# Scores of the first query block in one plain 32-bit product of 128 columns instead of three passes over 256

## The chip, the core and the metric

The kernel runs on one core of a Trainium2 chip. The metric is the device time of one execution in microseconds, as the median of several runs. Lower is better.

## What is computed

One transformer layer in 32-bit floats for 2 batches of 512 tokens of width 512. After a layer norm (`xn`) three things are added up: the input, the output of an attention, and the output of a mixture of experts with a shared expert. The attention has 32 query heads in 8 groups; each group of 4 shares one key and value head of size 128:

```python
q = q * cos + rotate_half(q) * sin          # the same for k
scores = einsum('bkgtd,bksd->bkgts', qg, k) / sqrt(128)
scores = where(causal, scores, -inf)
attn = softmax(scores, axis=-1)
out = einsum('bkgts,bksd->bkgtd', attn, v)  # then the product with Wo
```

The mask is causal, so queries 0 to 127 of a batch see keys 0 to 127 only. Each token also goes through 2 of 16 experts (512 to 128 and back), chosen by a router.

## The kernel before

The five engines run one instruction stream each and meet at semaphores; the order of each stream is written out by hand in its own function `key_head(g)`, which stands once for g = 0, as the body of a loop for g = 1 to 6, and once for g = 7. One key head means: 4 query heads of both batches (b = 0 and 1), the projections that the next steps need, and 4 or 5 tiles of 128 expert rows.

**Split products.** Most products are made from split operands. ScalarE (or GpSimd) writes the value rounded to the type fp32r (`_hi`), VectorE writes the rest (`_lo`), and TensorE adds three passes, lo x hi, hi x lo and hi x hi (`product`, line 1241). The experts' products (lines 1460 and 1477) are plain 32-bit ones: one call of matmul, which the trace shows as two records. The transpositions (lines 1369, 1395, 1450, 1469) are one record per call.

**Queries.** For one batch and head, TensorE projects q transposed (`project_q`, line 1323: 128 dimensions x 512 tokens) into the bank PROJ_BANK. VectorE multiplies it by the cosine and sine tables (`turn_q1`, `turn_q2`, lines 919 and 931; semaphore q_turned). GpSimd adds the two halves in place (`add_q`, line 429; q_summed). ScalarE writes q_hi (`hi_q`, line 579; q_hi_ok), VectorE q_lo (`lo_q`, line 939; q_split). The next `turn_q1` waits for q_summed and q_split, because the tile `rot` is used again. For the first batch of key head 0 the sum is made by VectorE (line 1024). The bank PROJ_BANK also takes the next key and value projection (`project_kv`, line 1345), which waits for q_turned of the head before.

**Keys.** `project_kv` gives keys and values, VectorE turns the keys (`turn_k`), GpSimd sums them (`add_k`), TensorE transposes them back into PROJ_BANK (`transpose_k`, line 1362), ScalarE writes kT_hi (`hi_kT`, line 594) and VectorE kT_lo (`lo_kT`, line 968; kT_split). Two places on TensorE wait for kT_split: the first scores of a batch, and the third query projection (h = 2, line 1335), which needs the bank back. In the order of TensorE that projection is line 1542 for b = 1 and line 1625 for b = 0 of the next head.

**Scores.** `scores(g, b, i, m)` (line 1372) makes the scores of query block i (128 queries) against the keys 0 to 128 (i + 1) - 1. Two heads share a bank for i = 0 and 1, one head has it for i = 2 and 3; each such share is a use, and the uses take turns between two banks. For i = 0 the kernel computes 256 columns of which 128 are read afterwards. Then VectorE adds the mask and takes the maximum (`maxima`, line 975), ScalarE makes the exponentials (`exps`, line 600), VectorE the inverse sums (line 985), GpSimd normalises (`normalise`, line 463), TensorE transposes the probabilities (`transpose_p`, line 1387; prob_ok), they are split (lines 624 and 1008), multiplied with the values (`values`, line 1399) and projected (`project_out`, line 1412).

The four uses of the first query block in a key head stand at lines 1486 and 1496 (b = 0) and 1559 and 1576 (b = 1) of TensorE's order. Around the first and third of them that order reads:

```python
project_q(g + 1, 0, 3, 3)      # 1642, the end of the loop body
values(g, 1, 2, 1)
values(g, 1, 2, 2)
scores(g, 0, 0, 0)             # 1486, the start of the next one
project_kv(g, 1, 0, 0)         # 1487
...
scores(g, 1, 0, 0)             # 1559
project_out(g, 0, 1, 0)
values(g, 0, 2, 2)
transpose_p(g, 0, 3, 0)        # 1562
```

Of the kernel before, what the change touches and what calls it, by code (L numbers as in the profile page):

```python
# [7 lines left out]
F32 = mybir.dt.float32  # L8
F32R = mybir.dt.float32r
BF16 = mybir.dt.bfloat16  # L10
I32 = mybir.dt.int32
ALU = mybir.AluOpType
ACT = mybir.ActivationFunctionType
AX_X = mybir.AxisListType.X

P = 128
B, T, D = 2, 512, 512
# [4 lines left out]
G = HEADS // KV  # L22
# [13 lines left out]
S_BANKS, MOE_BANK, PROJ_BANK, OUT_BANK, PT_BANKS, OT_BANK = (0, 1), 2, 3, 4, (5, 6), 7  # L36
# [5 lines left out]
SHARE = [((0, 1), (2, 3)), ((0, 1), (2, 3)), ((0,), (1,), (2,), (3,)), ((0,), (1,), (2,), (3,))]  # L42
USES = 12
USE0 = [0, 2, 4, 8]
# [10 lines left out]
def wait_count(eng, sem, value):  # L55

    if not isinstance(value, int) or value > 0:
        eng.wait_ge(sem, value)


def count(per_step, g, b, k):

    return (2 * per_step) * g + (per_step * b + k)
# [7 lines left out]
def no_head(g):  # L71

    return isinstance(g, int) and not 0 <= g < KV
# [7 lines left out]
def build(nc, x, wq, wkv, wo, shared, sb3, w12, w3, b12, b3, router_w, router_b, router_bias,  # L81
# [8 lines left out]
    with ExitStack() as ctx:  # L90
        def sb(name, shape, dt=F32, stack=ctx):
            return stack.enter_context(nc.sbuf_tensor(name, shape, dt))

        def sem(name):
            return ctx.enter_context(nc.semaphore(name))
# [13 lines left out]
        bank = [ctx.enter_context(nc.psum_tensor(f"bank{i}", [P, 512], F32)) for i in range(8)]  # L109
# [65 lines left out]
            wo_raw = sb("wo_raw", [P, G, D], stack=raws)  # L175
        wo_lo = sb("wo_lo", [P, G, D], F32R)
        wo_hi = sb("wo_hi", [P, G, D], F32R)
        q_hi = sb("q_hi", [P, B, G, T], F32R)
        q_lo = sb("q_lo", [P, B, G, T], F32R)
        kT_hi = sb("kT_hi", [P, B, T], F32R)  # L180
        kT_lo = sb("kT_lo", [P, B, T], F32R)
        v_hi = sb("v_hi", [P, B, TB, P], F32R)
        v_lo = sb("v_lo", [P, B, TB, P], F32R)
        rot = sb("rot", [P, 2, T])
# [35 lines left out]
        q_psum, q_turned, q_summed, q_hi_ok, q_split = (sem(n) for n in ("q_psum", "q_turned", "q_summed", "q_hi_ok", "q_split"))  # L220
# [169 lines left out]
        def _(pool):  # L390
# [38 lines left out]
            def add_q(g, b, h):  # L429

                if no_head(g):
                    return
                pool.wait_ge(q_turned, count(4, g, b, h + 1))
                wait_count(pool, q_split, count(4, g, b, h))
                nc.gpsimd.tensor_tensor(rot[:, 0, :], rot[:, 0, :], rot[:, 1, :], ALU.add).then_inc(q_summed, 1)  # L435

            def add_k(g, b, i):

# [112 lines left out]
        def _(act):  # L551
# [3 lines left out]
            for n in range(B * HC):  # L555
                c, b = n % HC, n // HC
# [4 lines left out]
            for j in range(B):  # L561
                last = nc.scalar.activation(lT[:, j * T:(j + 1) * T], bank[LT_BANKS[j]][0:E, :], ACT.Copy)
# [6 lines left out]
            for t in range(4):  # L569
                s, b = t % 2, t // 2  # L570
# [8 lines left out]
            def hi_q(g, b, h, turned=rot):  # L579
                if no_head(g):  # L580
                    return
                act.wait_ge(q_summed, count(4, g, b, h + 1))
                nc.scalar.activation(q_hi[:, b, h, :], turned[:, 0, :], ACT.Copy).then_inc(q_hi_ok, 1)

            def hi_v(g, b, i, at=PROJ_BANK):
                if no_head(g):
# [7 lines left out]
            def hi_kT(g, b, at=PROJ_BANK):  # L594
                if no_head(g):
                    return
                act.wait_ge(kT_psum, count(1, g, b, 1))
                nc.scalar.activation(kT_hi[:, b, :], bank[at][:, :], ACT.Copy).then_inc(kT_hi_ok, 1)

            def exps(g, b, i, m):  # L600
# [164 lines left out]
        def _(dve):  # L765
# [9 lines left out]
            for n in range(NB):  # L775
                dve.wait_ge(x_in[n], 16)
                last = nc.vector.bn_stats(stats[:, n, :], y[:, n, :])
            link(last)
            for n in range(NB):
                last = nc.vector.bn_aggr(mv[:, n, :], stats[:, n, :])  # L780
# [17 lines left out]
            for n in range(B * HC):  # L798
                c, b = n % HC, n // HC
# [131 lines left out]
            def turn_q2(g, b, h, at=PROJ_BANK, turned=rot):  # L931
                if no_head(g):
                    return

                q = bank[at]
                nc.vector.tensor_tensor(turned[0:64, 1, :], q[64:128, :], qs[64:128, :], ALU.mult)
                nc.vector.tensor_tensor(turned[64:128, 1, :], q[0:64, :], qs[0:64, :], ALU.mult).then_inc(q_turned, 1)  # L937

            def lo_q(g, b, h, turned=rot):
                if no_head(g):  # L940
                    return
                dve.wait_ge(q_hi_ok, count(4, g, b, h + 1))
                nc.vector.tensor_tensor(q_lo[:, b, h, :], turned[:, 0, :], q_hi[:, b, h, :].bitcast(F32), ALU.subtract)\
                    .then_inc(q_split, 1)

            def turn_k(g, b, i, at=PROJ_BANK):
# [68 lines left out]
            for h in range(G):  # L1015
                turned = first_rot[h % 2]
                turn_q1(0, 0, h, FIRST_Q_BANKS[h], turned)
                turn_q2(0, 0, h, FIRST_Q_BANKS[h], turned)
                if h > 0:
                    lo_q(0, 0, h - 1, first_rot[(h - 1) % 2])  # L1020
                if h == 2:
                    lo_kT(0, 0, FIRST_KT_BANK)
                dve.wait_ge(q_turned, h + 1)
                nc.vector.tensor_tensor(turned[:, 0, :], turned[:, 0, :], turned[:, 1, :], ALU.add).then_inc(q_summed, 1)
            lo_q(0, 0, TB - 1, first_rot[1])

            def last_lo_q(g, b):
# [212 lines left out]
        def _(pe):  # L1240
            def product(dst, terms, stop=True):

                for k, (a_hi, a_lo, c_hi, c_lo) in enumerate(terms):
                    nc.tensor.matmul(dst, a_lo, c_hi, start=k == 0, stop=False)  # L1244
                    nc.tensor.matmul(dst, a_hi, c_lo, start=False, stop=False)  # L1245
                    last = nc.tensor.matmul(dst, a_hi, c_hi, start=False, stop=stop and k == len(terms) - 1)  # L1246
                return last
# [3 lines left out]
            for n in range(B * HC):  # L1251
                c, b = n % HC, n // HC
                pe.wait_ge(xn_ready, TB * (b + 1))
                wait_count(pe, xT_ok, n - 3)
                for k in range(TB):
                    last = nc.tensor.transpose(bank[TR_BANKS[n % 4]][:, k * P:(k + 1) * P],
                                               xn[:, TB * b + k, c * P:(c + 1) * P], ident[:, :])
# [3 lines left out]
            for b in range(B):  # L1261
                span = slice(b * T, (b + 1) * T)
                last = product(bank[LT_BANKS[b]][0:E, :],
                               [(rw_hi[:, c, :], rw_lo[:, c, :], xT_hi[:, c, span], xT_lo[:, c, span])
                                for c in range(HC)])
# [105 lines left out]

            def scores(g, b, i, m):

                use, width = USE0[i] + m, max(256, P * (i + 1))
                if i == 0 and m == 0:
                    pe.wait_ge(kT_split, count(1, g, b, 1))
                if i == 0:
                    pe.wait_ge(q_split, count(4, g, b, SHARE[i][m][-1] + 1))
                wait_count(pe, exps_ok, count(USES, g, b, use - 1))
                cols = slice(i * P, (i + 1) * P)  # L1380
                for k, h in enumerate(SHARE[i][m]):
                    s = bank[S_BANKS[use % 2]]
                    last = product(s[:, 256 * k:256 * k + width],
                                   [(q_hi[:, b, h, cols], q_lo[:, b, h, cols], kT_hi[:, b, 0:width], kT_lo[:, b, 0:width])])
                last.then_inc(s_psum, 1)

            def transpose_p(g, b, i, j):
# [262 lines left out]
            last = (KV - 1, 1, TB - 1)  # L1650
# [85 lines left out]
```

## Time and profile before

| | us |
|---|---|
| median of 3 runs | 976.89 (973.25 to 977.38) |
| the profiled execution | 974.4 |
| span of its instructions | 972.6 |
| PE busy | 922.1 (95%) |
| PE weight loads busy | 772.5 (79%) |
| DVE busy | 678.7 (70%) |
| POOL busy | 391.5 (40%) |
| ACT busy | 377.3 (39%) |

PE is TensorE's matmuls and PEld its weight loads, which overlap them; DVE is VectorE, ACT ScalarE, POOL GpSimd, SP the queue that issues most DMAs. Matmuls are pipelined and their ends are modelled, so the duration of a record holds a latency that overlaps the next one. For how long a matmul keeps the engine, the distance between two starts is the figure to read. Register, branch and semaphore instructions are not counted as busy.

### The profile page before, as it was taken

The page shows a single profiled execution, that of the slowest core. Times are in us where ns is not written, and L with a number is a line of the kernel's source. Part 1 is how long each engine was busy: PE and PEld are TensorE (multiplying, and loading weights), DVE is VectorE, ACT ScalarE, POOL GpSimd, SP SyncE. Part 2 cuts the span into 40 slices and gives each one's busy share as a digit, 9 for nine tenths or more (in the row PEclk, how much of TensorE's full clock was granted, in tenths as well). Part 3 has the DMA queues.
Part 4 walks back from the last instruction along what each step waited for, and adds up shares of the span by engine and source line. Part 5 has one row for each costly group of instructions (what it writes and reads, how often), then busy time and mean ns, then how long its engine had stood idle before and what let it go on. Part 6 is the DMA issues. An engine that isn't in the chain of part 4 may idle for free.

```text
span 972.6 us, 16710 instructions
## 1 busy us (share of the span) xinstructions
PE 922.1 (95%) x4945; PEld 772.5 (79%) x4945; DVE 678.7 (70%) x1543; ACT 377.3 (39%) x997; POOL 391.5 (40%) x510
## 2 busy tenths in 40 slices
PE   2799799999999999999999999999999999999986
PEld 2477678887888888888888888888888988888864
DVE  7486785758665775768666585757767586657884
ACT  2111343435333443435434443335433453334532
POOL 5900277624352353324362253425343243423571
PEclk9989899999999999999999999999999999999999
DMA  9700221224233243215323142414423242321160
GB/s 323 279 0 1 77 76 65 101 73 149 82 96 89 81 145 110 84 42 166 105 87 96 54 151 91 125 38 145 127 84 92 64 144 77 114 70 55 43 186 32
DMA packets 51727, 97.70 MB, mean 100 GB/s; under 512 B 5872, under 2 KB 17776, under 8 KB 51696
## 3 DMA queue, kind: packets, MB, share of 16 engines
q1 hardware_dynamic: 49136, 88.94, 28.8%
q0 software_dynamic: 2560, 8.39, 2.7%
q8 instruction: 15, 0.25, 0.1%
q14 instruction: 16, 0.13, 0.0%
HBM read 74.76 MB, written 22.54 MB: 100 GB/s over the span
## 4 chain that ended last, share of the span: by engine, by line
PE 83%; DVE 11%; issue 2%; DMA 1%; POOL 1%; ACT 1%; SPq 0%; DVEq 0%; ACTq 0%; POOLq 0%
PE bank L1244 7%; PE bank L1246 7%; PE bank L1245 7%; PE bank L1395 6%; PE bank L1339 6%; PE bank L1423 6%; PE bank L1341 6%; PE bank L1340 6%; PE bank L1460 6%; PE bank L1425 6%; PE bank L1424 6%; PE bank L1408 3%; PE bank L1410 3%; PE bank L1409 3%; PE bank L1477 3%
## 5 line engine op out<-in xcount | busy, mean ns | idle before, releaser
L469 POOL TENSOR_SCALAR prob<-prob,rsum 128x128 f32<-128x128 f32 (+3 forms) x256 | 138.7, 560 | 307.7 <-DVE rsum L987 307.6
L624 ACT ACTIVATE pT_hi<-bank 128x512 fp32r<-128x512 f32 x160 | 94.7, 599 | 185.1 <-PE bank L1395 118.1
L605 ACT ACTIVATE prob<-bank,nmax 128x128 f32<-128x128 f32 (+3 forms) x256 | 133.0, 525 | 52.2 <-DVE nmax L981 52.2
L435 POOL TENSOR_TENSOR rot<-rot 128x512 f32<-128x512 f32 x60 | 77.2, 1287 | 171.3 <-DVE rot L937 171.3
L981 DVE CUSTOM_DVE_ANT_0 bank<-bank,causal 128x128 f32<-128x128 f32 (+3 forms) x256 | 122.0, 503 | 32.3 <-PE bank L1246 31.9
L1008 DVE TENSOR_TENSOR pT_lo<-bank,pT_hi 128x512 fp32r<-128x512 f32 x160 | 107.7, 683 | 45.8 <-ACT pT_hi L624 45.5
L1339 PE MATMUL bank<-xT_hi,wq_lo 128*128 128x512 f32 x256 | 109.9, 429 | 6.1 <-DVE v_lo L965 6.1
L1423 PE MATMUL bank<-wo_hi,oT_lo 128*128 128x512 f32 x256 | 109.2, 427 | 3.4 <-DVE oT_lo L993 2.8
L1341 PE MATMUL bank<-xT_hi,wq_hi 128*128 128x512 f32 x256 | 101.4, 396 | 0.0
L1340 PE MATMUL bank<-xT_lo,wq_hi 128*128 128x512 f32 x256 | 101.3, 396 | 0.0
L1425 PE MATMUL bank<-wo_hi,oT_hi 128*128 128x512 f32 x256 | 101.0, 395 | 0.0
L1424 PE MATMUL bank<-wo_lo,oT_hi 128*128 128x512 f32 x256 | 100.8, 394 | 0.0
L1244 PE MATMUL bank<-kT_hi,q_lo 128*128 128x256 f32 (+2 forms) x256 | 89.4, 349 | 3.1 <-ACT prob L605 2.1
L1395 PE MATMUL bank<-ident,prob 128*128 128x128 f32 x640 | 87.1, 274 | 3.9 <-POOL prob L469 3.7
L1395 PEld LDWEIGHTS bank<-ident,prob 128*128 128x128 f32 x640 | 73.9, 141 | 13.8 <-POOL prob L469 7.2
L1245 PE MATMUL bank<-kT_lo,q_hi 128*128 128x256 f32 (+2 forms) x256 | 82.9, 324 | 0.0
L1246 PE MATMUL bank<-kT_hi,q_hi 128*128 128x256 f32 (+2 forms) x256 | 82.9, 324 | 0.0
L1244 PE MATMUL bank<-wkv_hi,xT_lo 128*128 128x256 f32 x256 | 75.9, 297 | 2.2 <-DVE prob L937 1.6
L1245 PE MATMUL bank<-wkv_lo,xT_hi 128*128 128x256 f32 x256 | 72.3, 282 | 0.0
L1246 PE MATMUL bank<-wkv_hi,xT_hi 128*128 128x256 f32 x256 | 72.1, 282 | 0.0
L1408 PE MATMUL bank<-pT_hi,v_lo 128*128 128x512 f32 x160 | 66.8, 418 | 1.5 <-DVE pT_lo L1008 1.5
L615 ACT ACTIVATE oT_hi<-bank 128x512 fp32r<-128x512 f32 x64 | 38.3, 599 | 76.6 <-PE bank L1410 76.6
(183 smaller groups left out, 2025.6 us busy)
## 6 DMA issues: line engine op xcount, KB each, us to landing
w_raw<-w SPq DMA_DIRECT2D x31, 512.0 KB, 3.8
wq_raw<-wq SPq DMA_DIRECT2D x32, 256.0 KB, 3.3
wo_raw<-wo SPq DMA_DIRECT2D x32, 256.0 KB, 3.2
xg<-x_slots SPq DMA_DIRECT2D x31, 256.0 KB, 2.6
eb<-b SPq DMA_DIRECT2D x31, 256.0 KB, 4.3
w_raw<-w SPq DMA_DIRECT2D x31, 256.0 KB, 4.1
y_slots<-moe_y SPq DMA_DIRECT2D x31, 256.0 KB, 3.1
x_slots<-pairs SPq DMA_DIRECT2D x3, 2048.0 KB, 16.2
```

The costliest lines, as they stand in the source:

```text
L469: last = nc.gpsimd.tensor_scalar(row, row, rsum[:, G * i + h:G * i + h + 1], 1.0, ALU.mult, ALU.mult)
L605: last = nc.scalar.activation(prob[i % 2][:, h, 0:P * (i + 1)], bank[S_BANKS[use % 2]][:, 256 * k:256 * k + P * (i + 1)], ACT.Exp, bias=nm ...
L1244: nc.tensor.matmul(dst, a_lo, c_hi, start=k == 0, stop=False)
L1245: nc.tensor.matmul(dst, a_hi, c_lo, start=False, stop=False)
L1246: last = nc.tensor.matmul(dst, a_hi, c_hi, start=False, stop=stop and k == len(terms) - 1)
L1339: nc.tensor.matmul(q, wq_lo[:, h, col], xT_hi[:, c, span], start=c == 0, stop=False)
L1340: nc.tensor.matmul(q, wq_hi[:, h, col], xT_lo[:, c, span], start=False, stop=False)
L1341: last = nc.tensor.matmul(q, wq_hi[:, h, col], xT_hi[:, c, span], start=False, stop=c == HC - 1)
L1395: last = nc.tensor.transpose(bank[PT_BANKS[n % 2]][:, h * P:(h + 1) * P], prob[i % 2][:, h, j * P:(j + 1) * P], ident[:, :])
L1423: nc.tensor.matmul(dst, oT_lo[:, k, h], wo_hi[:, h, :], start=h == 0, stop=False)
L1424: nc.tensor.matmul(dst, oT_hi[:, k, h], wo_lo[:, h, :], start=False, stop=False)
L1425: last = nc.tensor.matmul(dst, oT_hi[:, k, h], wo_hi[:, h, :], start=False, stop=h == G - 1)
```

## The change

It gives the first query block its own operands, `q_first` and `k_first`, in plain 32-bit floats and 128 columns wide, and makes its scores in one matmul call per head of 128 x 128 x 128 instead of three passes over 256 columns. The sum of the turned query becomes two operations (the first 128 tokens into `q_first`, the other 384 in place), q_hi and q_lo shrink to 384 tokens, ScalarE makes one more copy per batch and key head, ahead of kT_hi, and the waits move: block 0 waits for q_summed, block 1 takes the wait for q_split.

```diff
--- before.py
+++ after.py
@@ -175,8 +175,10 @@
             wo_raw = sb("wo_raw", [P, G, D], stack=raws)
         wo_lo = sb("wo_lo", [P, G, D], F32R)
         wo_hi = sb("wo_hi", [P, G, D], F32R)
-        q_hi = sb("q_hi", [P, B, G, T], F32R)
-        q_lo = sb("q_lo", [P, B, G, T], F32R)
+        q_first = sb("q_first", [P, B, G, P])
+        k_first = sb("k_first", [P, B, P])
+        q_hi = sb("q_hi", [P, B, G, T - P], F32R)
+        q_lo = sb("q_lo", [P, B, G, T - P], F32R)
         kT_hi = sb("kT_hi", [P, B, T], F32R)
         kT_lo = sb("kT_lo", [P, B, T], F32R)
         v_hi = sb("v_hi", [P, B, TB, P], F32R)
@@ -432,7 +434,8 @@
                     return
                 pool.wait_ge(q_turned, count(4, g, b, h + 1))
                 wait_count(pool, q_split, count(4, g, b, h))
-                nc.gpsimd.tensor_tensor(rot[:, 0, :], rot[:, 0, :], rot[:, 1, :], ALU.add).then_inc(q_summed, 1)
+                nc.gpsimd.tensor_tensor(q_first[:, b, h, :], rot[:, 0, 0:P], rot[:, 1, 0:P], ALU.add)
+                nc.gpsimd.tensor_tensor(rot[:, 0, P:T], rot[:, 0, P:T], rot[:, 1, P:T], ALU.add).then_inc(q_summed, 1)
 
             def add_k(g, b, i):
 
@@ -580,7 +583,7 @@
                 if no_head(g):
                     return
                 act.wait_ge(q_summed, count(4, g, b, h + 1))
-                nc.scalar.activation(q_hi[:, b, h, :], turned[:, 0, :], ACT.Copy).then_inc(q_hi_ok, 1)
+                nc.scalar.activation(q_hi[:, b, h, :], turned[:, 0, P:T], ACT.Copy).then_inc(q_hi_ok, 1)
 
             def hi_v(g, b, i, at=PROJ_BANK):
                 if no_head(g):
@@ -595,6 +598,7 @@
                 if no_head(g):
                     return
                 act.wait_ge(kT_psum, count(1, g, b, 1))
+                nc.scalar.activation(k_first[:, b, :], bank[at][:, 0:P], ACT.Copy)
                 nc.scalar.activation(kT_hi[:, b, :], bank[at][:, :], ACT.Copy).then_inc(kT_hi_ok, 1)
 
             def exps(g, b, i, m):
@@ -940,7 +944,7 @@
                 if no_head(g):
                     return
                 dve.wait_ge(q_hi_ok, count(4, g, b, h + 1))
-                nc.vector.tensor_tensor(q_lo[:, b, h, :], turned[:, 0, :], q_hi[:, b, h, :].bitcast(F32), ALU.subtract)\
+                nc.vector.tensor_tensor(q_lo[:, b, h, :], turned[:, 0, P:T], q_hi[:, b, h, :].bitcast(F32), ALU.subtract)\
                     .then_inc(q_split, 1)
 
             def turn_k(g, b, i, at=PROJ_BANK):
@@ -1021,7 +1025,9 @@
                 if h == 2:
                     lo_kT(0, 0, FIRST_KT_BANK)
                 dve.wait_ge(q_turned, h + 1)
-                nc.vector.tensor_tensor(turned[:, 0, :], turned[:, 0, :], turned[:, 1, :], ALU.add).then_inc(q_summed, 1)
+                nc.vector.tensor_tensor(q_first[:, 0, h, :], turned[:, 0, 0:P], turned[:, 1, 0:P], ALU.add)
+                nc.vector.tensor_tensor(turned[:, 0, P:T], turned[:, 0, P:T], turned[:, 1, P:T], ALU.add)\
+                    .then_inc(q_summed, 1)
             lo_q(0, 0, TB - 1, first_rot[1])
 
             def last_lo_q(g, b):
@@ -1371,17 +1377,22 @@
 
             def scores(g, b, i, m):
 
-                use, width = USE0[i] + m, max(256, P * (i + 1))
+                use, width = USE0[i] + m, P * (i + 1)
                 if i == 0 and m == 0:
                     pe.wait_ge(kT_split, count(1, g, b, 1))
                 if i == 0:
+                    pe.wait_ge(q_summed, count(4, g, b, SHARE[i][m][-1] + 1))
+                if i == 1:
                     pe.wait_ge(q_split, count(4, g, b, SHARE[i][m][-1] + 1))
                 wait_count(pe, exps_ok, count(USES, g, b, use - 1))
-                cols = slice(i * P, (i + 1) * P)
+                cols = slice((i - 1) * P, i * P)
                 for k, h in enumerate(SHARE[i][m]):
-                    s = bank[S_BANKS[use % 2]]
-                    last = product(s[:, 256 * k:256 * k + width],
-                                   [(q_hi[:, b, h, cols], q_lo[:, b, h, cols], kT_hi[:, b, 0:width], kT_lo[:, b, 0:width])])
+                    s = bank[S_BANKS[use % 2]][:, 256 * k:256 * k + width]
+                    if i == 0:
+                        last = nc.tensor.matmul(s, q_first[:, b, h, :], k_first[:, b, :], start=True, stop=True)
+                    else:
+                        last = product(s, [(q_hi[:, b, h, cols], q_lo[:, b, h, cols],
+                                            kT_hi[:, b, 0:width], kT_lo[:, b, 0:width])])
                 last.then_inc(s_psum, 1)
 
             def transpose_p(g, b, i, j):
```

## Rows read from the trace of the kernel before

**Rows 1.** The page: busy time, share of the span, instructions; the chain that ended last.

```profile
PE 922.1 (95%) x4945; PEld 772.5 (79%) x4945; DVE 678.7 (70%) x1543; ACT 377.3 (39%) x997; POOL 391.5 (40%) x510
...
PE 83%; DVE 11%; issue 2%; DMA 1%; POOL 1%; ACT 1%; SPq 0%; DVEq 0%; ACTq 0%; POOLq 0%
```

**Rows 2.** Busy time by stretches of the span (window, its length, engines, clock, DMA).

```profile
420.00:530.00 110.00, 109.92 (x600) 93.14 (x599) 75.86 (x179) 46.00 (x125) 41.29 (x56) 1.00 0.31 98
```

**Rows 3.** Timeline at line 1486, key head 3: start, us, engine, operation [idle before <-releaser].

```profile
416.32 0.69 DVE L929 TENSOR_TENSOR rot<-bank,qc 128x512 f32<-128x512 f32 x1 [1.02 <-PE bank L1341]
...
417.51 0.28 PE L1244 MATMUL bank<-kT_hi,q_lo 128*128 128x256 f32 x1
417.51 0.19 PEld L1245 LDWEIGHTS bank<-kT_lo,q_hi 128*128 128x128 f32 x1
...
417.63 0.19 PEld L1246 LDWEIGHTS bank<-kT_hi,q_hi 128*128 128x128 f32 x1
417.73 0.68 DVE L937 TENSOR_TENSOR rot<-bank,qs 64x512 f32<-64x512 f32 x1
...
418.11 0.28 PE L1246 MATMUL bank<-kT_hi,q_hi 128*128 128x256 f32 x1
...
418.46 0.19 PEld L1244 LDWEIGHTS bank<-wkv_hi,xT_lo 128*128 128x128 f32 x1 [0.28 <-DVE rot L937]
418.46 0.39 PE L1244 MATMUL bank<-wkv_hi,xT_lo 128*128 128x256 f32 x1
...
418.69 0.29 PE L1245 MATMUL bank<-wkv_lo,xT_hi 128*128 128x256 f32 x1
```

**Rows 4.** TensorE's instructions grouped by line and form: count | busy us, mean ns | idle.

```profile
L1395 PE MATMUL bank<-ident,prob 128*128 128x128 f32 x640 | 87.1, 274 | 3.9 <-POOL prob L469 3.7
...
L1460 PE MATMUL bank<-w_raw,xgT 128*128 128x256 f32 x248 | 59.7, 383 | 0.0
...
L1460 PEld LDWEIGHTS bank<-w_raw,xgT 128*128 128x128 f32 x248 | 45.5, 189 | 8.2 <-ACT xgT L650 2.1
```

**Rows 5.** Timeline: the experts' up projection, eight records in one.

```profile
422.66 1.89 PE L1460 MATMUL bank<-w_raw,xgT 128*128 128x256 f32 x8
```

**Rows 6.** Timeline around the keys of the second batch, key head 3 (lines 1536 to 1542).

```profile
452.56 1.28 POOL L435 TENSOR_TENSOR rot<-rot 128x512 f32<-128x512 f32 x1 [1.15 <-DVE rot L937]
...
453.65 1.04 PE L1395 MATMUL bank<-ident,prob 128*128 128x128 f32 x8
453.85 0.60 ACT L650 ACTIVATE xgT<-bank 128x512 f32<-128x512 f32 x1 [5.46 <-PE bank L1450]
...
454.34 0.59 ACT L598 ACTIVATE kT_hi<-bank 128x512 fp32r<-128x512 f32 x1
...
454.82 0.63 ACT L583 ACTIVATE q_hi<-rot 128x512 fp32r<-128x512 f32 x1
...
454.97 0.69 DVE L972 TENSOR_TENSOR kT_lo<-bank,kT_hi 128x512 fp32r<-128x512 f32 x1 [0.58 <-ACT kT_hi L598]
...
455.71 0.19 PEld L1339 LDWEIGHTS bank<-xT_hi,wq_lo 128*128 128x128 f32 x1
```

**Rows 7.** The other engines' instructions grouped by line and form.

```profile
L435 POOL TENSOR_TENSOR rot<-rot 128x512 f32<-128x512 f32 x60 | 77.2, 1287 | 171.3 <-DVE rot L937 171.3
...
L943 DVE TENSOR_TENSOR q_lo<-rot,q_hi 128x512 fp32r<-128x512 f32 x62 | 52.0, 838 | 13.8 <-ACT q_hi L583 13.7
...
L442 POOL TENSOR_TENSOR ksum<-krot 128x256 f32<-128x256 f32 x32 | 23.8, 742 | 36.1 <-DVE krot L957 36.1
...
L667 ACT ACTIVATE hT<-bank 128x128 f32<-128x128 f32 x31 | 8.5, 275 | 0.0
```

**Rows 8.** Timeline at line 1562, key head 3.

```profile
466.63 3.13 POOL L469 TENSOR_SCALAR prob<-prob,rsum 128x512 f32<-128x512 f32 x4 [1.24 <-DVE rsum L987]
...
469.97 0.37 PEld L1395 LDWEIGHTS bank<-ident,prob 128*128 128x128 f32 x2
```

**Rows 9.** Who waited for whom: total us, times, longest us.

```profile
ACT q_hi L583 <- POOL rot L435: 5.6, 8, 0.8
```

## What the change does to the time: the prediction

> **What bounds the kernel now.** I read the page first. TensorE is busy 95% of the span and the chain that ended last lies on it for 83% [rows 1]. That busy share overstates the load, since ends are modelled, so I took the table by stretches next: in the steady key heads PE is busy 109.92 of 110.00 us, the weight loads 93.14, and VectorE (75.86), ScalarE (46.00) and GpSimd (41.29) have room; the granted clock there is 1.00, which is the 2.4 GHz level [rows 2]. The reader is to see a kernel bound by the order of work on TensorE, with the other engines idle a third of the time or more. The last view is the timeline of one steady key head (the one that runs from about 418 to 529 us), read for the places where TensorE's next instruction waits for another engine. There are few: the largest is 0.28 us [rows 3]. So TensorE work removed should come off the end, except inside a stretch that a fixed path through another engine covers. The question is how much TensorE time goes, and how many of the places lie in such a stretch.
>
> **TensorE: what goes and what comes.** The scores of the first query block are 64 head products (2 batches, 32 heads), issued two by two in 32 uses of a bank, four per key head (lines 1486, 1496, 1559, 1576). Today each head is three instructions of 256 columns. A record shows 0.28 to 0.30 us but they overlap; what counts is the distance of starts: from 417.51 to 418.11 us are five distances, 0.12 each [rows 3]. A use of six records occupies 0.72 us.
>
> A plain 32-bit product appears in the trace as two records per call: the experts' up projection has 248 for its 31 x 4 calls, 383 ns mean [rows 4]. A group of 8 takes 1.89 us [rows 5]; less one record of 0.383 that leaves 1.51 for 7 distances, 0.215 each. Half the columns give 0.108. Eight 128-column transposes, also from 32-bit data, take 1.04 us, and less one record's 0.274 that is 0.109 per record [rows 4, 6]. So the new head is 2 x 0.109 = 0.22 us, and a use 0.44 instead of 0.72: 0.28 us saved. Weight loads could spoil this: a plain load's record is 189 ns long [rows 4]. But loads of 0.19 us start every 0.12 us under the present passes [rows 3], so 0.12 per record is the near bound: a use of 0.48, saving 0.24. The far bound is in the rivals. I take 0.28, since nothing shows a load limit at 0.12 rather than the streaming. All 32 uses: 9.0 us, or 7.7 at the near bound.
>
> **The use at line 1486 gives nothing.** The following key and value projection (line 1487) writes the projection bank and waits until VectorE has turned the last query head. VectorE starts at 416.32, having waited for TensorE's projection, needs three operations of 0.69 and ends at 418.41; the load for line 1487 starts at 418.46 after 0.28 idle [rows 3]. That path starts ahead of the score product and does not contain it, so a shorter product is only a longer wait. Eight uses, 8 x 0.28 = 2.2 us, are lost. The others leave 24 x 0.28 = 6.7 us.
>
> **The new copy of the keys.** ScalarE writes k_first ahead of kT_hi, 16 times. A 128-column copy out of PSUM takes 275 ns; successive ScalarE records overlap by 0.10 (an operation of 0.60 at 453.85, the next at 454.34), so kT_hi comes 0.17 later [rows 6, 7]. For the second batch that chain is tight: kT_hi at 454.34, kT_lo on VectorE from 454.97 to 455.66, and the load of the third query projection (line 1542) at 455.71, 0.05 after its release [rows 6]. It has perhaps 0.07 of play, as a load runs ahead of its matmul. A wait also costs more than itself: after the one at 418.46 the next record starts 0.23 later where 0.12 is usual [rows 3]. So 0.10 + 0.10 = 0.20 us per key head, 1.6 in all; bounds 0 (the shorter q_lo, queued ahead, gives it back) and 0.3 x 8 = 2.4. Behind kT_lo on VectorE queue q_lo and the maxima of the last query block, which have more room. For the first batch line 1625 comes later in the order and I cost the copy at nothing.
>
> **The next wait uncovered.** After the use at line 1559 comes the transposition of the last block's probabilities (line 1562). GpSimd ends normalising them at 466.63 + 3.13 = 469.76, the load starts at 469.97 [rows 8]. TensorE 0.28 earlier would be there 0.07 before the release, plus 0.05 for the signal: some 0.1 us, 0.8 in all (bounds 0 and 0.25 x 8 = 2.0). The uses at lines 1496 and 1576 have no releaser that close behind, other than ones whose own source lies after the use and moves with it.
>
> **The small edits.** GpSimd's sum of the turned query becomes two operations. From 256 columns at 742 ns and 512 at 1287, an operation has 197 fixed, so the split costs 0.20 us, 60 times [rows 7]. I cost it at nothing: the sum that ends at 452.56 + 1.28 = 453.84 is read by ScalarE at 454.82, nearly 1 us later [rows 6], and ScalarE waited for that sum 8 times, 5.6 us in all [rows 9]. Going the other way, q_hi and q_lo lose 128 of 512 columns, about 0.1 of 0.63 and 0.2 of 0.84 us [rows 6, 7], mostly off the path. The same split on VectorE in the prologue (4 times, under 0.1 each) is paid by the shorter q_lo. The first block's scores wait for the sum instead of the split, which comes earlier; the second block takes over the wait for the split and is behind it already. Nothing is moved on SP and no DMA changes.
>
> **Sum.** 6.7 - 1.6 - 0.8 = 4.3, less 0.3 for the first and last key heads, where TensorE waits for others more: 4.0 us. The profiled execution took 974.4 (span 972.6): 970.4. The median of three runs is 976.89, 2.5 above it, which would give 972.9. Between the two I say 971.5. That is 0.4%, just under the 0.5% that can be told from no change here (about 4.9 us).
>
> **The rivals.** (1) All three open uses reach the end, because the shorter q_lo and q_hi repay the copy and line 1562: -6.7, 967.7 to 970.2 by the two baselines. For: GpSimd, ScalarE and VectorE have room [rows 2]. Against: the 0.05 at line 1542 [rows 6]. Chance 0.22.
>
> (2) The gain melts: every kept use runs into some wait on VectorE within the key head, as at line 1487. Then only the copy is felt, -1 to +1.6, some 976. For: VectorE's waits stand close behind TensorE's in the order. Against: only 0.08 us of 110 is idle [rows 2]. Chance 0.13.
>
> (3) Slower through the sum on GpSimd: if each of the 60 sums passed its 0.20 to q_split and so to VectorE's next turn, 12 us stand against 6.7, +5.3, 979.7 to 982. It decides once ScalarE reaches q_hi less than 0.2 us after the sum; the trace shows 1 us [rows 6]. Chance 0.05.
>
> (4) Slower through weight loads: if a plain 128-column record had to pay its load openly, it costs 0.189 + 0.109 = 0.30, a head 0.60 instead of 0.36, and 64 heads +15 us, about 991. It decides at 0.18 per record. The experts' records hide such loads under 0.215, and the present passes under 0.12 [rows 3, 5]. Chance 0.05. The Trainium skill (TensorE: Matmul & The Clock Gate, Part 3, The mechanism) says that a load overlaps running matmuls only where the row group differs; with 107 ns per load of 128 columns (its section LDWEIGHTS, an estimate from its P / 1.2) a head would be 4 x 107 = 0.43 and the change a loss of some 4.5 us. By that rule the present passes of full height could not be 0.12 apart with a load each, so the trace contradicts it.
>
> **How the numbers follow.** The forecast case, -1.5 to -6.5 us, has 0.55; about 0.18 of it lies beyond -4.9. With rival 1 that makes faster 0.40. Same: 0.37 + 0.13 = 0.50. Slower: 0.10. The range runs from rival 1 on the lower baseline, 967.7, less 1.2 for the spread of the runs (the lowest, 973.25, against 974.4), so 966, to rival 2 with the full price of the copy on the upper baseline, 976.89 + 1.6, so 979. Rivals 3 and 4 lie outside it, with the far tails of the others.
>
> **What would show it.** Right: the first block's records as 128 matmuls of 128 columns, about 0.11 apart and 0.44 per use; the wait at line 1487's load grown from 0.28 to about 0.55; a wait of 0.1 to 0.2 on kT_lo at the third query projection; a period of key heads shorter by about 0.5 us (0.84 - 0.20 - 0.10). Wrong: records 0.2 or more apart; a period unchanged or shorter by 0.8; ScalarE's q_hi waiting for GpSimd far more than 8 times.

## The result and the profile after

The changed kernel takes 970.89 us (median of 20 runs, 968.62 to 974.52) against 974.85 for the kernel before (20 runs beside them, 970.96 to 977.38). The ratio is 0.9962, 95% interval 0.9951 to 0.9973: about 3.7 us faster. The profiled execution took 969.35, its span is 967.6. Of all executions below one, of pool_twice, fell into a slower state (1036.41 us at a granted clock of 0.845, where the others have 0.98 to 1.00) and is left out of its ratio.

The page of the changed kernel, busy times and the chain (before: [rows 1]):

```profile
PE 913.9 (94%) x4881; PEld 762.9 (79%) x4881; DVE 672.7 (70%) x1547; ACT 373.2 (39%) x1013; POOL 395.9 (41%) x570
...
PE 80%; DVE 13%; issue 3%; ACT 2%; DMA 1%; POOL 1%; SPq 0%; DVEq 0%; ACTq 0%; another core or an unknown queue 0%; POOLq 0%
```

TensorE has 64 records fewer (192 passes gone, 128 come), and the chain has moved a little from TensorE to VectorE and ScalarE. The groups by line and form of the changed kernel show the new instructions (before: [rows 4, 7]):

```profile
L1392 PE MATMUL bank<-k_first,q_first 128*128 128x128 f32 x128 | 19.5, 274 | 0.7 <-DVE kT_lo L976 0.7
L1392 PEld LDWEIGHTS bank<-k_first,q_first 128*128 128x128 f32 x128 | 19.0, 190 | 3.6 <-DVE kT_lo L976 1.1
...
L437 POOL TENSOR_TENSOR q_first<-rot 128x128 f32<-128x128 f32 x60 | 27.8, 464 | 174.4 <-DVE rot L941 174.4
...
L438 POOL TENSOR_TENSOR rot<-rot 128x384 f32<-128x384 f32 x60 | 60.6, 1010 | 0.0
...
L947 DVE TENSOR_TENSOR q_lo<-rot,q_hi 128x384 fp32r<-128x384 f32 x62 | 46.5, 750 | 12.1 <-ACT q_hi L586 11.9
...
L601 ACT ACTIVATE k_first<-bank 128x128 f32<-128x128 f32 x16 | 4.4, 274 | 38.9 <-PE bank L1375 38.9
```

The timeline of the changed kernel at the start of key head 3 (before: [rows 3]):

```profile
416.56 0.69 DVE L933 TENSOR_TENSOR rot<-bank,qc 128x512 f32<-128x512 f32 x1 [1.26 <-PE bank L1347]
...
417.75 0.61 PE L1392 MATMUL bank<-k_first,q_first 128*128 128x128 f32 x4
417.97 0.68 DVE L941 TENSOR_TENSOR rot<-bank,qs 64x512 f32<-64x512 f32 x1
...
418.71 0.19 PEld L1250 LDWEIGHTS bank<-wkv_hi,xT_lo 128*128 128x128 f32 x1 [0.54 <-DVE rot L941]
...
418.93 0.29 PE L1251 MATMUL bank<-wkv_lo,xT_hi 128*128 128x256 f32 x1
```

Four records take 0.61 us; less one record of 0.274, three distances are 0.112 each. The wait of the key and value projection has grown from 0.28 to 0.54 us: what the shorter product gave is in it.

At the three other uses the gain stays. I compared, position by position in TensorE's order, the starts in both traces from the second to the last key head: at the instruction behind each of these uses the changed kernel moves ahead by 0.28 (line 1496), 0.26 to 0.27 (line 1559) and 0.27 us (line 1576), in every head. The distance between key heads shows it too. These are the loads with which key head 1 and key head 7 begin, first in the kernel before, then in the changed one:

```profile
193.86 0.19 PEld L1244 LDWEIGHTS bank<-kT_hi,q_lo 128*128 128x128 f32 x1
...
862.97 0.19 PEld L1244 LDWEIGHTS bank<-kT_hi,q_lo 128*128 128x128 f32 x1
```

```profile
195.65 0.19 PEld L1392 LDWEIGHTS bank<-k_first,q_first 128*128 128x128 f32 x1
...
859.68 0.19 PEld L1392 LDWEIGHTS bank<-k_first,q_first 128*128 128x128 f32 x1
```

A sixth of the difference is the period of a key head: 111.52 us before, 110.67 after, 0.85 less. I use this period below, as it leaves out the first and the last head, where single profiles scatter: in the kernels of this study that share the old product (before, fill_before, width128) the first head alone took 98.4 to 100.7 us.

### The profile page after: what moved, and what is told of

It is laid out like the page before. It is cut to its first block, busy times and chain, and to the rows that moved or that the text cites. A ratio compares the mean times of both kernels' runs of the same rounds, so it can differ in the third digit from the quotient of the medians.

```text
span 967.6 us, 16670 instructions
## 1 busy us (share of the span) xinstructions
PE 913.9 (94%) x4881; PEld 762.9 (79%) x4881; DVE 672.7 (70%) x1547; ACT 373.2 (39%) x1013; POOL 395.9 (41%) x570
## 4 chain that ended last, share of the span: by engine, by line
PE 80%; DVE 13%; issue 3%; ACT 2%; DMA 1%; POOL 1%; SPq 0%; DVEq 0%; ACTq 0%; another core or an unknown queue 0%; POOLq 0%
PE bank L1250 7%; PE bank L1252 7%; PE bank L1251 6%; PE bank L1406 6%; PE bank L1471 6%; PE bank L1434 6%; PE bank L1436 5%; PE bank L1435 5%; PE bank L1345 5%; PE bank L1347 5%; PE bank L1346 5%; PE bank L1419 3%; PE bank L1421 3%; PE bank L1420 3%; PE bank L1488 3%
## 5 line engine op out<-in xcount | busy, mean ns | idle before, releaser
L472 POOL TENSOR_SCALAR prob<-prob,rsum 128x128 f32<-128x128 f32 (+3 forms) x256 | 136.7, 554 | 296.7 <-DVE rsum L991 296.6
L437 POOL TENSOR_TENSOR q_first<-rot 128x128 f32<-128x128 f32 x60 | 27.8, 464 | 174.4 <-DVE rot L941 174.4
L1250 PE MATMUL bank<-kT_hi,q_lo 128*128 128x256 f32 (+2 forms) x192 | 71.9, 374 | 3.7 <-issue 2.0
L1345 PEld LDWEIGHTS bank<-xT_hi,wq_lo 128*128 128x128 f32 x256 | 48.6, 190 | 20.9 <-DVE v_lo L969 8.2
L1252 PE MATMUL bank<-kT_hi,q_hi 128*128 128x256 f32 (+2 forms) x192 | 64.8, 337 | 0.0
```

The source lines that it names most:

```text
L472: last = nc.gpsimd.tensor_scalar(row, row, rsum[:, G * i + h:G * i + h + 1], 1.0, ALU.mult, ALU.mult)
L1345: nc.tensor.matmul(q, wq_lo[:, h, col], xT_hi[:, c, span], start=c == 0, stop=False)
```

## The experiments

Each ran in five rounds (width128 in three) against the kernel before. "Ratio" is to that kernel, "period" the mean of six key heads of one profiled execution, from the same two loads as above. The kernels ran in three groups, in which the kernel before had medians of 974.29 (after_again, both twice kernels, fill_after), 974.76 (copy_twice, no_copy, pool_twice, long_split) and 974.08 us (the others); across groups the ratio is the figure to compare.

| kernel | median us | ratio (95% interval) | period us |
|---|---|---|---|
| before | 974.85 | | 111.52 |
| changed | 970.89 | 0.9962 (0.9951 to 0.9973) | 110.67 |
| after_again | 969.36 | 0.9949 (0.9929 to 0.9969) | 110.63 |
| twice_at_wait | 967.55 | 0.9929 (0.9907 to 0.9951) | 110.93 |
| twice_at_open | 971.13 | 0.9967 (0.9951 to 0.9982) | 111.12 |
| fill_after | 965.23 | 0.9902 (0.9880 to 0.9923) | 110.10 |
| copy_twice | 969.58 | 0.9953 (0.9935 to 0.9971) | 110.94 |
| no_copy | 969.47 | 0.9947 (0.9930 to 0.9963) | 110.60 |
| pool_twice | 972.93 | 0.9975 (0.9962 to 0.9988) | 111.01 |
| long_split | 974.71 | 0.9999 (0.9985 to 1.0012) | 111.18 |
| long_swap | 973.40 | 0.9996 (0.9981 to 1.0011) | 110.96 |
| fill_swap | 966.99 | 0.9934 (0.9915 to 0.9952) | 110.18 |
| fill_before | 971.33 | 0.9975 (0.9961 to 0.9989) | 111.25 |
| width128 | 974.00 | 0.9992 (0.9977 to 1.0006) | 111.44 |

**The control, after_again.**

> The changed kernel itself, as the control for the three that run with it. My theory: three of the four first-block uses per key head shorten the time, the one ahead of the key and value projection only lengthens a wait, so 3.5 to 4.5 us under the kernel before.

969.36 us; ratio 0.9949, so 5.0 us under the kernel before, the period 110.63. Changed kernel and control together stand for 3.7 to 5.0.

**Does the use at the start of the head count?**

```diff
+                        for _ in range(2 if (b, m) == (0, 0) else 1):
                             last = nc.tensor.matmul(s, q_first[:, b, h, :], k_first[:, b, :], start=True, stop=True)
```

> Each product of the use at the start of the key head (b = 0, heads 0 and 1) is issued twice, 0.44 us more of TensorE work in each of 8 key heads, the result unchanged. My theory: the wait for VectorE that follows has grown to 0.54 us and takes it up, so the time stays within 0.8 us of the changed kernel and the wait in the profile falls to 0.1. The rival, that TensorE's work is what counts everywhere: 8 x 0.44 = 3.5 us slower than the changed kernel.

967.55 us, not slower than the control: 3.5 us of added TensorE work cost nothing in the time. Its timeline at the same place:

```profile
416.02 1.05 PE L1393 MATMUL bank<-k_first,q_first 128*128 128x128 f32 x8
...
416.98 0.19 PEld L1250 LDWEIGHTS bank<-wkv_hi,xT_lo 128*128 128x128 f32 x1
```

Eight records now, and the load behind them carries no wait mark (a row has one above 0.15 us). The rival (3.5 us slower than the control) is outside the interval. The period is 0.3 above the control's, though, 1.8 us in six key heads. Most of it is the wait for late weights told of at the end; TensorE's waits of 200 to 860 us, the control first:

```profile
PEld bank L1250 <- ACT prob L609: 0.7, 1, 0.7
```

```profile
PEld bank L1250 <- ACT prob L609: 2.2, 3, 1.6
```

**The same work at an open use.**

```diff
+                        for _ in range(2 if (b, m) == (1, 0) else 1):
                             last = nc.tensor.matmul(s, q_first[:, b, h, :], k_first[:, b, :], start=True, stop=True)
```

> The same doubling at the first use of the second batch (heads 0 and 1), where my theory sees no wait behind it: 3.5 us slower than the changed kernel, 3.0 to 3.8 with the small play at the transposition behind it. A rival by which gains and losses there melt into later waits on VectorE: under 1.5 us.

971.13 us, 1.8 over the control, period + 0.49 for 0.44 of work. Position by position all of the 0.45 appears right behind the doubled product. The time, half of the 3.5 expected with an interval of about 2.4 either way, doesn't tell the theories apart alone; the trace speaks for the open use. Against twice_at_wait it is 3.6 us.

**Is the wait real idle time?** The transpositions of the last block's probabilities are ready 2 us before, so they can stand in it.

```diff
                 scores(g, 0, 0, 0)
-                project_kv(g, 1, 0, 0)
                 transpose_p(g - 1, 1, 3, 0)
                 transpose_p(g - 1, 1, 3, 1)
+                project_kv(g, 1, 0, 0)
```

> The changed kernel with the eight transpositions of the last block's probabilities (0.87 us, released 2 us before) issued ahead of the key and value projection instead of behind it, so that TensorE works while VectorE turns the last query. My theory: the 0.54 us wait and the 0.1 that follows a wait go, 8 x 0.55 to 0.65 = 4.4 to 5.2 us faster than the changed kernel. The rival: the key and value projection or its readers are on a path of their own (VectorE's queue), and the wait shows up at the values or the first query projection: under 1.5 us.

965.23 us, 4.1 under the control, a little less than the 4.4 to 5.2 expected and far from the rival; period - 0.53. The timeline:

```profile
416.34 0.61 PE L1392 MATMUL bank<-k_first,q_first 128*128 128x128 f32 x4
...
416.78 1.04 PE L1406 MATMUL bank<-ident,prob 128*128 128x128 f32 x8
...
417.55 0.19 PEld L1250 LDWEIGHTS bank<-wkv_hi,xT_lo 128*128 128x128 f32 x1
```

TensorE does not wait between the three. This is the fastest kernel of the study: ratio 0.9902. The same edit on the kernel before:

> The kernel before with only the transpositions ahead of the key and value projection. Its wait there is 0.28 us and the 0.1 behind it: 8 x 0.37 = 3.0 us faster than before, 971 to 972. If my theory of the wait is wrong, under 1 us.

971.33 us, 2.7 under its runs beside it, ratio 0.9975, so 2.4 by the ratio against 3.0 expected. The smaller wait gives the smaller gain, in line with the theory.

**The copy of the keys, made twice** (the first time into a spare tile) **and left out.**

```diff
+                nc.scalar.activation(k_spare[:, b, :], bank[at][:, 0:P], ACT.Copy)
                 nc.scalar.activation(k_first[:, b, :], bank[at][:, 0:P], ACT.Copy)
```

> The changed kernel with the 128-column copy of the keys made a second time into a spare tile, ahead of the first: kT_hi and kT_lo 0.17 us later, 16 times, the result unchanged. The step of my prediction (0.2 us per key head once the play is used up) gives 1.4 to 2 us slower than the changed kernel. The theory after reading its trace, that the projection waiting for kT_lo is reached 0.13 us or more after it: 0.3 to 1 us.

969.58 us, ratio 0.9953: within the intervals that is the changed kernel. Its trace is not. The period is 0.3 longer than the changed kernel's and its control's (110.94 against 110.67 and 110.63), and a wait has grown; TensorE's waits of 200 to 860 us, the changed kernel first, then copy_twice:

```profile
PEld bank L1345 <- DVE v_lo L969: 1.2, 6, 0.2
```

```profile
PEld bank L1347 <- DVE v_lo L971: 2.7, 12, 0.4
```

So a second copy does reach TensorE, in the one profiled execution (974.79 us, the slowest of the seven). Whether it costs time in the median is not shown.

```diff
-                nc.scalar.activation(k_first[:, b, :], bank[at][:, 0:P], ACT.Copy)
...
-                        last = nc.tensor.matmul(s, q_first[:, b, h, :], k_first[:, b, :], start=True, stop=True)
+                        last = nc.tensor.matmul(s, q_first[:, b, h, :], kT_hi[:, b, 0:P].bitcast(F32), start=True, stop=True)
```

> The changed kernel without the copy of the keys: the product reads the rounded kT_hi as plain 32-bit floats, so the first block's scores lose the low part of the keys. If the copy costs what I predicted, 1.6 us faster than the changed kernel; by the trace, where nothing waits for kT_lo, 0 to 0.5.

969.47 us, ratio 0.9947, period 110.60 against 110.63 to 110.67. The interval of the time alone would still allow the 1.6 us; the period, 0.03 to 0.07 shorter, does not. The first copy costs next to nothing. The timeline of the changed kernel at that place (before: [rows 6]) tells why:

```profile
453.33 1.41 DVE L1041 TENSOR_TENSOR wo_lo<-wo_raw,wo_hi 128x512 fp32r<-128x512 f32 x1
...
454.45 0.27 ACT L601 ACTIVATE k_first<-bank 128x128 f32<-128x128 f32 x1
454.61 0.60 ACT L602 ACTIVATE kT_hi<-bank 128x512 fp32r<-128x512 f32 x1
...
454.79 0.19 PEld L1434 LDWEIGHTS bank<-wo_hi,oT_lo 128*128 128x128 f32 x1 [0.24 <-DVE wo_lo L1041]
...
455.24 0.69 DVE L976 TENSOR_TENSOR kT_lo<-bank,kT_hi 128x512 fp32r<-128x512 f32 x1 [0.50 <-ACT kT_hi L602]
...
456.06 0.19 PEld L1345 LDWEIGHTS bank<-xT_hi,wq_lo 128*128 128x128 f32 x1
```

kT_hi starts 0.16 after the copy, as reckoned. But in this head TensorE is held just before, 0.24 us, by the split of an output weight, and then reaches the projection (456.06) 0.13 after kT_lo is done (455.93). Two waits that stand one behind the other are paid once. In the kernel before, key head 3, which I had read, has no such hold and only 0.05 between kT_lo and the load [rows 6]; key heads 2, 4, 5 and 6 are not like it. Key head 2 of the kernel before:

```profile
343.48 0.69 DVE L972 TENSOR_TENSOR kT_lo<-bank,kT_hi 128x512 fp32r<-128x512 f32 x1 [0.41 <-ACT kT_hi L598]
...
344.42 0.19 PEld L1339 LDWEIGHTS bank<-xT_hi,wq_lo 128*128 128x128 f32 x1
```

The load comes 0.25 after kT_lo is done, and 0.20 to 0.23 after it in key heads 4, 5 and 6: room for the 0.17 of the copy. In the changed kernel that room is used up: in key heads 2, 5 and 6 the load comes 0.05 to 0.06 after kT_lo, but the matmul behind it starts, counted from the first load of the key head, at most 0.03 later than in no_copy.

**GpSimd's sum, made longer.**

```diff
+                nc.gpsimd.tensor_tensor(q_spare[:, h, :], rot[:, 0, 0:P], rot[:, 1, 0:P], ALU.add)
                 nc.gpsimd.tensor_tensor(q_first[:, b, h, :], rot[:, 0, 0:P], rot[:, 1, 0:P], ALU.add)
```

> The changed kernel with GpSimd's first 128-column sum made twice (0.46 us more, 60 times, into a spare tile, result unchanged). My theory: ScalarE comes to the sum 0.9 us after it, so under 1 us slower than the changed kernel, all of it through VectorE being slowed while GpSimd works. The rival of the prediction, that the sums reach VectorE's turns: 5 us and more of 28.

972.93 us, ratio 0.9975: some 2.5 over the changed kernel by the ratios of it and its control, the period 0.34 to 0.38 longer. More than my "under 1", less than the rival's 5. The waits of ScalarE and TensorE show where; first the changed kernel, then pool_twice:

```profile
ACT q_hi L586 <- POOL rot L438: 7.7, 8, 1.0
...
PEld bank L1471 <- ACT xgT L654: 2.9, 11, 0.3
```

```profile
PEld bank L1473 <- ACT xgT L656: 5.4, 12, 0.6
...
ACT q_hi L588 <- POOL rot L440: 12.0, 10, 1.5
...
PEld bank L1347 <- DVE kT_lo L978: 1.5, 6, 0.2
```

ScalarE has to wait for the sum of the fourth query of the second batch, and behind that rounding in its queue stands the copy of the expert's rows, for which TensorE's up projection waits. Against the control that projection comes 0.4 us later in each of key heads 1 to 6, all of the longer period. The waits for kT_lo are new too, but cost nothing: where they stand, the wait for wo_lo just ahead of them is gone.

**The shorter split undone in time.**

```diff
+                nc.scalar.activation(q_pad[:, b, 0, :], turned[:, 0, 0:P], ACT.Copy)
                 nc.scalar.activation(q_hi[:, b, h, :], turned[:, 0, P:T], ACT.Copy).then_inc(q_hi_ok, 1)
...
+                nc.vector.tensor_tensor(q_pad[:, b, 1, :], turned[:, 0, 0:P], turned[:, 0, 0:P], ALU.subtract)
                 nc.vector.tensor_tensor(q_lo[:, b, h, :], turned[:, 0, P:T], q_hi[:, b, h, :].bitcast(F32), ALU.subtract)
```

> The changed kernel with the shortening of the query split undone in time: ScalarE and VectorE each make one more 128-column operation per head into a spare tile (0.17 and 0.2 us, 64 times; result unchanged). If the shorter split is what paid for the copy of the keys, 1 to 2 us slower than the changed kernel, with a wait on kT_lo or on the turned query in the profile. If VectorE has room there, under 0.7 us.

974.71 us, ratio 0.9999: all of the gain is gone, 4 to 5 us, more than either theory allowed. The waits I had named are not there. What grew most is that chain through ScalarE again; the timeline of long_split at the up projection of the third tile:

```profile
473.94 0.31 ACT L587 ACTIVATE q_pad<-rot 128x128 f32<-128x128 f32 x1 [1.23 <-POOL rot L439]
...
474.15 0.51 ACT L588 ACTIVATE q_hi<-rot 128x384 fp32r<-128x384 f32 x1
...
474.57 0.58 ACT L656 ACTIVATE xgT<-bank 128x512 f32<-128x512 f32 x1
...
475.20 1.59 PEld L1474 LDWEIGHTS bank<-w_raw,xgT 128*128 128x128 f32 x8 [0.55 <-ACT xgT L656]
```

GpSimd's sum, ScalarE's pad and rounding, the copy, and TensorE idle for 0.55 us. The pad is an operation of its own and so costs more than the columns the change took off; the run overstates what the shorter split saved, but shows that it was no free term.

**That chain cut.** The next kernel tests it, on the same lengthened split:

```diff
-                last_hi_q(g, 1)
                 copy_xg(tile_of(g, 2))
+                last_hi_q(g, 1)
```

> The kernel with the lengthened query split (long_split), and on ScalarE the copy of the expert's rows (third tile) ahead of the rounding of the fourth query head, not behind it. The trace of long_split shows 0.42 us of its loss per key head at the experts' up projection of that tile, which waits for this copy, which stands behind a rounding that waits for GpSimd's sum. If that chain is the price, 3 to 3.5 us come back: 971 to 972, the key heads 110.7 to 110.8 us apart instead of 111.2. If VectorE's longer split is the price, the wait reappears at the next product and the time stays above 973.5.

973.40 us, ratio 0.9996, a miss. The named wait went back to its old size, and the period fell by 0.22, half of the 0.42:

```profile
PEld bank L1474 <- ACT xgT L656: 2.1, 6, 0.3
```

Totals of this wait are 5.4 us in long_split and 2.1 here. By the ratios the time came down by 0.3 us, which the intervals can't tell from nothing. So this chain is one part of the price of the longer split. Position by position against the control, long_split loses 0.4 us at this up projection in each of key heads 2 to 6 and 0.10 to 0.14 some 88 us into it, where the first load of an output projection waits for oT_lo, which VectorE writes; together that is nearly all of its 0.55 us of longer period. In long_split, key head 3:

```profile
506.23 0.19 PEld L1437 LDWEIGHTS bank<-wo_hi,oT_lo 128*128 128x128 f32 x1 [0.16 <-DVE oT_lo L1000]
```

This second place stays in long_swap in most key heads, so VectorE's part of the longer split has a price as well. Waits of 0.1 to 0.2 on the probabilities and on the output weight's split are longer or more frequent in both traces too. Why the median of long_swap shows none of the 0.22 per key head that its period gives back is open.

> Both orders at once on the changed kernel: the transpositions ahead of the key and value projection (fill_after), and ScalarE's copy of the expert's rows ahead of the fourth query head's rounding. In the changed kernel that second chain costs about 0.1 us per key head, so 0.5 to 1.5 us under fill_after, some 964; the rival, that the next wait takes it, gives the same as fill_after.

966.99 us, ratio 0.9934 against 0.9902, period 110.18 against 110.10: nothing gained over fill_after. In the changed kernel the chain was not worth cutting. By the two ratios this kernel is even 3 us slower, at the edge of what the intervals allow while the periods are nearly equal; so the gain of fill_after may be nearer 3 us than 4.

**Fewer columns alone.**

```diff
-                use, width = USE0[i] + m, max(256, P * (i + 1))
+                use, width = USE0[i] + m, P * (i + 1)
```

> The kernel before with three passes over 128 columns for the first block instead of 256, the result unchanged. No row shows such a pass. If it streams at the rate of the longer ones, 0.06 us per record or 0.11 if the weight load bounds it: 0.18 to 0.33 us per head instead of 0.36, 1 to 8 us faster. If so short a pass runs at the rate of the plain product or slower (0.22 and more per record), 0.66 per head and 64 x 0.3 = 19 us slower, less the 2.4 that the first wait hides.

974.00 us, ratio 0.9992 (0.9977 to 1.0006): 0.8 us faster, not to be told from nothing, and far from the 19 slower. The timeline of this kernel at one use:

```profile
420.00 0.27 PE L1245 MATMUL bank<-kT_lo,q_hi 128*128 128x128 f32 x1
420.11 0.28 PE L1246 MATMUL bank<-kT_hi,q_hi 128*128 128x128 f32 x1
420.22 0.27 PE L1244 MATMUL bank<-kT_hi,q_lo 128*128 128x128 f32 x1
420.33 0.28 PE L1245 MATMUL bank<-kT_lo,q_hi 128*128 128x128 f32 x1
420.44 0.28 PE L1246 MATMUL bank<-kT_hi,q_hi 128*128 128x128 f32 x1
```

The records are 0.11 us apart, where those of 256 columns were 0.12 [rows 3]. That is the upper price of my first case, for which I had said 1 us faster. Halving the columns of a rounded pass gives back next to nothing; the change saves because it has two records per head instead of three.

## Why the prediction was right, and which of its terms were not

I forecast -4.0 us and 971.5; measured are -3.7 by the ratio (-5.0 in the control) and 970.89.

- **The price of the new product** held: 0.112 per record against 0.109, no load limit, so rival 4 is out. A use takes 0.44 to 0.45 us, and 0.26 to 0.28 came off where 0.28 was said.
- **The use at line 1486** gives nothing, as said: the wait grew by 0.26 us, doubling the product was free, and work moved into the wait came off the time. This is the best supported step.
- **The other three uses** reach the end. 3 x 0.27 = 0.81 against a period shorter by 0.85; I had forecast 0.5 for the period after the two costs below, and had named "a period unchanged or shorter by 0.8" as a sign of being wrong. By that sign the sum for the middle heads was wrong, though the total was right.
- **The copy of the keys** was mis-sized: 1.6 us forecast, nothing found in no_copy's period and trace. The delay of 0.17 was right; that it would reach TensorE was not. I had taken the play from key head 3, where it is 0.05; in four other key heads it is 0.20 to 0.25, in three of them because TensorE is held by wo_lo just before. The expected wait of 0.1 to 0.2 on kT_lo does not show. By the trace of copy_twice a second copy would not have been free.
- **Line 1562** I put at 0.8 us. The load there is released just in time now (in key head 3 GpSimd is done at 470.01, the load starts at 470.06), but no loss of 0.1 shows in the period. Together with the copy, 2.4 us of cost were forecast that did not come.
- **GpSimd's longer sum**, costed at nothing because ScalarE came 1 us later in the head I read, does lie on a path at one place, the fourth query of the second batch. Its wait total went from 5.6 [rows 9] to 7.7 us. In the changed kernel ScalarE's shorter rounding (526 ns, before 0.63 us [rows 6]) covers about half of the 0.2. I had looked at one place in the key head and spoken for all eight.
- **The shorter split**, which I called mostly off the path, was worth more than I said: lengthened again, the gain was gone. How much it is worth by itself is not shown, since that run makes the split longer than it was.
- **First and last key head** I put at -0.3. By the period, 8 x 0.85 = 6.8 us should have come, and 3.7 to 5.0 did, so some 2 to 3 us are missing outside the six middle heads. The profiles say the same: outside them passed 303.5, 304.5 and 304.0 us in the three with the old product (before, fill_before, width128) and 303.6, 304.9 and 304.3 in the changed kernel, its control and no_copy. One part of the loss is shown. In the first key head TensorE stands 6 us for VectorE's v_lo. The first load of the head and the load behind that wait, in the kernel before and then in the changed one:

```profile
95.47 0.19 PEld L1244 LDWEIGHTS bank<-kT_hi,q_lo 128*128 128x128 f32 x1 [1.34 <-DVE kT_lo L972]
...
122.23 0.29 PEld L1339 LDWEIGHTS bank<-xT_hi,wq_lo 128*128 128x128 f32 x1 [6.02 <-DVE v_lo L965]
```

```profile
96.26 0.52 PEld L1392 LDWEIGHTS bank<-k_first,q_first 128*128 128x128 f32 x4 [1.13 <-DVE kT_lo L976]
...
123.29 0.28 PEld L1345 LDWEIGHTS bank<-xT_hi,wq_lo 128*128 128x128 f32 x1 [6.17 <-DVE v_lo L969]
```

  That is 26.76 us before and 27.03 after: neither of the two uses up to there gains anything, and some 0.2 is lost. The other profiles with the same granted clock at this place agree (width128 26.80; twice_at_wait, fill_swap and long_split 26.97 to 27.01). The chain that TensorE waits for there runs over VectorE, where the sum in two parts now stands too; I had called that split paid by the shorter q_lo. Which of its operations makes the 0.2 was not tested. The rest, in the last key head above all, is open. That the total agreed is luck: the costs I overstated and the loss I did not see are of one size.

  Part of the scatter of the first head is TensorE's clock. The stretch from 96 to 106 us, first in the changed kernel, then in its control, the same program (the last three figures: granted clock, share and GB/s of the DMA):

```profile
96.00:106.00 10.00, 7.15 (x41) 6.67 (x42) 7.10 (x23) 3.67 (x9) 0.00 (x0) 0.83 0.01 2
```

```profile
96.00:106.00 10.00, 7.68 (x39) 7.28 (x39) 6.24 (x18) 3.52 (x8) 0.00 (x0) 0.66 0.00 0
```

  Shortly before and in it TensorE waits for VectorE, 1.13 and 2.15 us in the changed kernel, and then it has the lower level (1.2 GHz) for a while. In all fourteen profiles the way from the first load of the head to that of line 1516 takes 14.8 to 14.9 us where the granted clock of this stretch is 0.83, and 15.7 to 15.8 where it is 0.66. The profiles of the kernel before and of the changed one both have 0.83, so this does not explain the difference between them.

Of the rivals, the first (-6.7, everything reaches the end) describes the middle heads better than my forecast did; it is the total that fits mine.

## What to carry to other kernels

A matmul saved ahead of a wait whose own path starts before it saves nothing, but it shows a hole: look for ready work to put there, which was worth 0.5 us per key head here, beside the 0.85 of the change itself. Count records before columns when a product is small: two plain ones beat three rounded ones of the same or twice the width. Read a play in several rounds of a loop, not in one. And follow a helper's every place in the loop, with what is queued behind it on its engine, before calling a longer operation free.

## What had not been expected of the hardware

A rounded (fp32r) pass over 128 columns occupies TensorE for 0.11 us, the same as a plain record of 128 columns (0.112) and nearly as long as a rounded one over 256 (0.12). Whether the stream or the weight load sets this is not told by these runs.

ScalarE's queue holds exponentials behind the rounding of an output weight that arrives by DMA. In the kernel before ScalarE waits for one such weight in each of the eight key heads, 2.4 to 3.8 us, but in key heads 1 to 6 TensorE stands only behind the three longest of these waits: 0.68 us behind 3.47, 0.58 behind 3.37 and 0.16 behind 2.96, for the scores of the third block, and not at all behind 2.47 to 2.87. The 0.28 that the prediction calls the largest wait is that of the one key head it read. The two heads that stand longest also have the longest periods, 111.96 and 111.85 us against 111.17 to 111.46 in the others. Key head 4:

```profile
554.69 0.63 ACT L642 ACTIVATE wo_hi<-wo_raw 128x512 fp32r<-128x512 f32 x1 [3.37 <-DMA wo_raw<-wo]
555.23 0.56 ACT L605 ACTIVATE prob<-bank,nmax 128x384 f32<-128x384 f32 x1
...
555.93 0.19 PEld L1244 LDWEIGHTS bank<-kT_hi,q_lo 128*128 128x128 f32 x1 [0.58 <-ACT prob L605]
```
